# The front block of a fused convolution-attention kernel: angle tables in pieces, a third slot for x, weights issued by ScalarE, and some loads behind the change of blocks

## The reference

```python
xn = _gn(x)                                   # (4, 48, 48, 128), groups of 4 channels
q = xn @ Wq + bq
k = (xn @ Wk + bk) * scaling                  # scaling = 16 ** -0.5
v = xn @ Wv + bv
lepe = depthwise_conv_5x5(v, dw_w) + dw_b
qr = q * cos + rot(q) * sin                   # rot: pairs (a, b) -> (-b, a); cos, sin: (48, 48, 16), one table for all 8 heads
kr = k * cos + rot(k) * sin
attn = einsum("bhnm", qr, kr) + mask          # mask: (8 heads, 2304, 2304), the same for the 4 images
out = softmax(attn) @ v + lepe
x = x + out @ Wo + bo
```

## Time and profile before

| | us |
|---|---|
| median of three runs (lowest, highest) | 3610.34 (3608.89, 3616.03) |
| the profiled execution | 3615.75 |
| its span | 3614.0 |
| front block, from the span's start to the core's first DMA | 168.0 |
| core's first DMA to the first exponential | 13.7 |

### The profile page before, as it was taken

The page is one execution under the profiler, slowest core; times in us unless marked ns, Lnnn a source line. Parts: engine busy times, 40 slices in busy tenths (PEclk is TensorE's granted clock), DMA queues, the critical chain, the costliest instruction groups (busy, mean ns, idle before and its releaser), DMA issues. The chain is left out here.

```text
span 3614.0 us, 96388 instructions
## 1 busy us (share of the span) xinstructions
PE 3426.4 (95%) x30672; PEld 2653.5 (73%) x30672; DVE 2623.8 (73%) x6490; ACT 2029.5 (56%) x3660; POOL 1639.8 (45%) x854
## 2 busy tenths in 40 slices
PE   6599999999999999999999999999399999999988
PEld 4377777777777777777777777777277787877867
DVE  6588888888888888888888888888365564644457
ACT  3366666666666666666666666666145444454533
POOL 4565566565665565556655656566100100005112
PEclk9799999999999999999999999999699999999989
DMA  6732242224224224223322322221511020100011
GB/s 201 243 101 93 91 125 78 93 98 129 67 100 126 94 66 135 91 94 93 109 91 98 103 94 91 99 68 63 167 42 56 24 74 6 37 1 1 1 41 42
DMA packets 111321, 309.50 MB, mean 86 GB/s; under 512 B 11496, under 2 KB 72859, under 8 KB 90299
## 3 DMA queue, kind: packets, MB, share of 16 engines
q1 hardware_dynamic: 111195, 307.85, 27.4%
HBM read 253.49 MB, written 54.31 MB: 85 GB/s over the span
## 5 line engine op out<-in xcount | busy, mean ns | idle before, releaser
L747 DVE CUSTOM_DVE_ANT_0 c_S<-c_Sps,mask_tiles 128x768 f32<-128x768 f32 x1728 | 1619.5, 956 | 425.1 <-PE c_Sps L798 367.0
L688 ACT ACTIVATE c_PT<-c_Tps 128x512 f32<-128x512 f32 x2592 | 1428.7, 605 | 872.0 <-PE c_Tps L809 809.4
L659 POOL TENSOR_SCALAR c_S<-c_S,c_row_max 128x2304 f32<-128x2304 f32 x576 | 1410.9, 2450 | 949.4 <-DVE c_row_max L758 949.4
L809 PE MATMUL c_Tps<-ident,c_S 128*128 128x128 f32 x10368 | 1399.5, 273 | 4.1 <-ACT c_PT L688 4.1
L809 PEld LDWEIGHTS c_Tps<-ident,c_S 128*128 128x128 f32 x10368 | 1226.0, 140 | 151.4 <-ACT c_PT L688 9.9
L798 PE MATMUL c_Sps<-c_K,c_Q 96*128 (+1 forms) x3456 | 853.5, 328 | 43.5 <-DVEq L728 26.3
L822 PE MATMUL c_Ops<-c_PT,c_V 128*32 128x256 f32 x10368 | 619.1, 382 | 0.8 <-ACT c_PT L688 0.8
L822 PEld LDWEIGHTS c_Ops<-c_PT,c_V 128*32 128x32 f32 x10368 | 307.4, 109 | 243.7 <-issue 49.9
L798 PEld LDWEIGHTS c_Sps<-c_K,c_Q 96*128 96x128 bf16 x3456 | 315.0, 98 | 202.7 <-issue 144.4
L1313 DVE TENSOR_SCALAR_CACHE_REDUCE l_S<-l_Sps 128x384 f32<-128x384 f32 x432 | 240.2, 557 | 294.5 <-PE l_Sps L1161 268.2
L1081 ACT ACTIVATE ln2T<-l_Tps 128x384 f32<-128x384 f32 x432 | 196.4, 491 | 403.9 <-PE l_Tps L1182 403.9
(11 more groups left out here) (197 smaller groups left out, 1652.2 us busy)
## 6 DMA issues: line engine op xcount, KB each, us to landing
mask_tiles<-in_mask SPq DMA_DIRECT2D x144, 1152.0 KB, 7.7
numerators<-c_O SPq DMA_DIRECT2D x288, 64.0 KB
ln<-numerators SPq DMA_DIRECT2D x8, 2304.0 KB, 8.4
q_parts<-f_parts SPq DMA_DIRECT2D x12, 576.0 KB, 7.7
k_parts<-f_parts SPq DMA_DIRECT2D x12, 576.0 KB
c_Q<-q_parts SPq DMA_DIRECT2D x71, 96.0 KB
c_vpad<-v_padded SPq DMA_DIRECT2D x8, 756.0 KB, 14.8
c_K<-k_parts SPq DMA_DIRECT2D x7, 864.0 KB, 8.8
```

The costliest lines, as they stand in the source:

```text
L659: pool.tensor_scalar(S[:, slot, :], S[:, slot, :], -1.0, row_max[:, slot:slot + 1], ALU.mult, ALU.add).then_inc(shifted, 1)
L688: act.activation(dst, src, ACT.Exp, scale=-1.0).then_inc(exp_done, 1)
L747: dve.tensor_tensor_reduce(out=S[:, r % ROW_SLOTS, cols(CH, c)].rearrange("p (k n) -> p k n", k=2), in0=Sps[:, n % S_SLOTS, :, 0:GW], in1= ...
L809: last = pe.transpose(Tps[:, g % T_SLOTS, cols(P, k)], S[:, (2 * b + t) % ROW_SLOTS, cols(P, kt)], ident[:, :])
```

## The change

Six edits, all in the front and at the core's start.

1. `XT` has three slots, and x of images 0, 1 and 2 is loaded at the start; x of image 3 when the matmuls of image 0 are done. Each image's x has a semaphore of its own.
2. The angle tables come from the host already repeated for the eight heads, as 128 rows, and are loaded in three pieces each, 384 KB a piece, cos and sin in turn. `with_cos` waits for its own piece.
3. The weights, biases and taps are issued by ScalarE.
4. Two mask tiles and the first-head loads of image 2 leave the front; the core's start issues them. The first-head loads of images 0 and 1 stand half an image later, behind vpad (and behind x of image 3).
5. The statistics are two BN_STATS in each of steps 0, 1 and 2; deviation is in step 3 and normalise in step 4.
6. In the core, TensorE's rows 4 and 6 wait for the loads of image 2 and 3, and ScalarE's second `place_v` for both.

```diff
-        XT = sb("XT", [P, 2, N])
+        X_SLOTS = 3
+        XT = sb("XT", [P, X_SLOTS, N])
@@ front, SyncE
             load_x(0)
-            for i, w in enumerate((a["Wq"], None, a["Wk"], None, a["Wv"])):
...
-            sp.dma_start(cosT[:, :], s["cosT"].unsqueeze(0).to_broadcast([HEADS, D, N])).then_inc(angles_in, 16)
-            sp.dma_start(sinT[:, :], s["sinT"].unsqueeze(0).to_broadcast([HEADS, D, N])).then_inc(angles_in, 16)
+            for c in range(NCH):
+                sp.dma_start(cosT[:, cols(CH, c)], s["cosT"][:, cols(CH, c)]).then_inc(angles_in[c], 16)
+                sp.dma_start(sinT[:, cols(CH, c)], s["sinT"][:, cols(CH, c)]).then_inc(angles_in[c], 16)
             load_x(1)
+            load_x(2)
             for b in range(B):
                 if b:
                     store_parts(b - 1, 1)
                 store_v(b)
-                if b:
-                    load_early(b - 1)
-                sp.dma_start(mask[:, b, :], s["mask"][b]).then_inc(mask_in, 16)
+                if b < 2:
+                    sp.dma_start(mask[:, b, :], s["mask"][b]).then_inc(mask_in, 16)
                 store_parts(b, 0)
                 store_vpad(b)
-                if b + 2 < B:
+                if b + X_SLOTS < B:
                     sp.wait_ge(mm_ready, 2 * STEPS * (b + 1))
-                    load_x(b + 2)
+                    load_x(b + X_SLOTS)
+                if b in (1, 2):
+                    load_early(b - 1)
@@ front, ScalarE: the eight DMAs of weights, biases and taps ahead of its first wait
+                    act.dma_start(weights[:, i, :], w).then_inc(weights_in, 16)
...
-                    if step == STEPS - 2 and b + 1 < B:
+                    if step == 3 and b + 1 < B:
                         deviation(b + 1)
@@ front, VectorE
             def with_cos(u):
                 b, m, c = at(u)
+                if u < NCH:
+                    dve.wait_ge(angles_in[c], 32)
...
-            dve.wait_ge(angles_in, 32)
...
-                    if b + 1 < B and step == STEPS - 1:
+                    if b + 1 < B and step == 4:
                         normalise(b + 1)
                     with_sin(u)
-                    if b + 1 < B and step in (1, 2):
-                        statistics(b + 1, range(NG // 2 * (step - 1), NG // 2 * step))
+                    if b + 1 < B and step < 3:
+                        statistics(b + 1, range(2 * step, 2 * step + 2))
@@ core, SyncE
-            sp.sem_inc(mask_in, 32 * 2)
+            sp.sem_inc(mask_in, 32)
...
+            load_first_head(sp, s, K, Q, V_next, 2, [image_in[2]] * 3)
             load_half(0)
-            load_first_head(sp, s, K, Q, V_next, B - 1, (k_in, q_in, v_in))
-            sp.wait_ge(q_in, 48)
+            load_first_head(sp, s, K, Q, V_next, 3, [image_in[3]] * 3)
+            load_mask(1)
             load_q(1)
@@ core, ScalarE and TensorE
+                elif half:
+                    act.wait_ge(image_in[2], 16 * EARLY_LOADS)
+                    act.wait_ge(image_in[3], 16 * EARLY_LOADS)
...
+                if first and c == 0 and r in (4, 6):
+                    pe.wait_ge(image_in[r // 2], 16 * EARLY_LOADS)
@@ host
-    "cosT": lambda x: x.reshape(N, D).T,
+    "cosT": lambda x: np.tile(x.reshape(N, D).T, (HEADS, 1)),
```

More of the change, by code:

```diff
@@ L356, in v_tokens @@
                 for k in range(GB):
-                    last = pe.matmul(to[:, cols(P, k)], XT[:, b % 2, cols(P, g * GB + k)], weights[:, 4, :],
+                    last = pe.matmul(to[:, cols(P, k)], XT[:, b % X_SLOTS, cols(P, g * GB + k)], weights[:, 4, :],
                                      start=True, stop=True)
@@ L373, in project @@
                 for k in range(2):
[L374 removed]
+                    last = pe.matmul(mm[:, use % MM_SLOTS, k, 0:GW], weights[:, 2 * m + r, :], XT[:, b % X_SLOTS, cols(GW, 2 * c + k)],
                                      start=True, stop=True)
@@ L789, in scores @@
             def scores(ip, p, r, c, first=False):
-                if c == 0 and r == (ROWS - 2 if first else 0):
+                if r == 0 and c == 0 and not first:
                     pe.wait_ge(q_in, 48 * (ip + 1))
                     pe.wait_ge(k_in, 48 * (ip // HEAD_PAIRS + 1))
+                if first and c == 0 and r in (4, 6):
+                    pe.wait_ge(image_in[r // 2], 16 * EARLY_LOADS)
                 n = NCH * r + c
```

42 lines of the change are left out of this document (23 added, 19 removed).

## The result

| | us |
|---|---|
| before, median of four runs (lowest, highest) | 3612.63 (3608.89, 3616.03) |
| changed kernel, median of four runs (lowest, highest) | 3589.63 (3587.29, 3591.86) |
| ratio (95% interval) | 0.9936 (0.9919 to 0.9954) |
| profiled executions, before and after | 3615.75 and 3587.29 |

The change saves 23.0 us; 31 were forecast. The time, 3589.63, is at the upper end of the range, inside it.

The account below looks back on a forecast made before the run. It took late angle tables, waits for x and normalised x, TensorE's rhythm and the store tail to bound the front. 14 + 1.4 + 10.4 + 0 + 6.5 - 1 = 31.3, said 31, off 3610.34: 3579.3 us, range 3571 to 3590.

Parts of the forecast that it names:

- The start: Up to TensorE's third step: tables and x arrive sooner, 14 us less; bounds of the gain 5 and 14.3.
- The pieces: Table loads at the start: fixed parts of pieces overlap, against the skill's 1 MiB rule, which would cost some 3 us.
- Image 0: End of image 0: TensorE's wait for the normalised x goes, 1.4 us less.
- Images 1 and 2: Front's middle images: fewer stalls, 30.3 us becomes 25.5 and 32.1 becomes 26.5, 10.4 less.
- Image 3: Last image of the front: 24.6 us as before, 0 gained.
- The tail: Last matmul to the core's first DMA: moved loads no longer stand there, 6.5 us less, 25.9 becomes 19.4.
- The core's start: After the core's first DMA: vpad lands behind seven issues and VectorE waits, 1 us more; bounds 0 and 5.
- (a): Rival, 24%: eight DMA engines carrying all of k set the front's length; gain 25.5 us, 3585.
- (b): Rival, 12%: x or weights come late at the start, 9 us of it lost; gain 22 us, 3588.
- (c): Rival, 12%: better, images at 24.5 us and the tail less by 9; gain 37 us, 3573.
- (d): Rival, 8%: the core's start gives back 5 us; 3583.
- (e): Rival, 2%: slower, moved loads set the core's start, landing 30 us late, which cancels all.

Follow-up runs that it names:

- e11: e7 with weights, biases and taps issued by SyncE, behind x of image 0 and ahead of the table pieces; 3570.33 us.
- e3: Changed kernel with the tables still in pieces but broadcast by the DMA, 8 heads outermost; 3603.6 us.
- e1: Changed kernel with k laid out in HBM part outermost, so a store is 128 rows on sixteen DMA engines; 3575.29 us.
- e2: Changed kernel with the first-head loads of images 0 and 1 another half image later, behind V of the next image; 3589.0 us.
- e5: Changed kernel with statistics back in steps 1 and 2, deviation in step 4 and normalise in step 5; 3592.8 us.
- e9: Changed kernel with two slots for x instead of three, so x of images 2 and 3 is loaded later; 3607.48 us.
- e12: Changed kernel with two slots for x and also the old, later places of statistics, deviation and normalise; 3599.32 us.
- e4: Changed kernel with two mask tiles and the first-head loads of image 2 back in the front; 3598.8 us.
- e8: e1 with two mask tiles and the first-head loads of image 2 back in the front; 3574.5 us.
- e7: e1 with the core's first DMAs reordered: vpad's half and V of images 2 and 3 first; 3570.29 us.
- e6: e1 with statistics back in steps 1 and 2, deviation in step 4 and normalise in step 5; 3581.4 us.
- e10: e7 with the tables in pieces but broadcast by the DMA, 8 heads outermost; 3580.0 us.

## Why the prediction was right or wrong

**The start: right.** 14 were forecast, 13.2 came (24.15 at the third step, not 23.1). The missing 0.8 is the first projection, 1.1 us later than before. I had the weights sharing engines with x "within a microsecond either way"; e11 shows that they share with the table pieces. The bound below (x late behind slow tables) is what e3 measured at the third step; with the slow step behind it it was 11.5 us, not 8 to 9.

**The pieces: right.** The DMA view of the first 20 us in 40 slices (busy tenths, then GB/s), of the changed kernel:

```profile
DMA  0009159999999999999999999999999999940000
GB/s 0 0 0 111 19 193 350 418 405 399 419 387 377 423 400 398 386 407 408 393 399 393 399 390 442 424 424 396 396 424 424 433 378 406 424 175 0 0 0 0
```

About 400 GB/s from 3.5 us on, with table pieces of 384 KB in it. The Trainium skill's rule of 1 MiB a DMA for 75% of peak (DMA: Bandwidth & Descriptors, Measured (HBM→SBUF, 128 partitions, SWDGE, issued from GpSimd)) rests on DMAs issued by GpSimd. It doesn't hold for these pieces, which SyncE issues one behind another.

**Image 0: right.** 1.4 forecast, 1.2 came. Edit 5's worth is far more than the 1.4 of that place: 4.4 in all with edit 1.

**Images 1 and 2: wrong in image 2.** Image 1 took 24.7 where I said 25.5; image 2 took 30.9 where I said 26.5. The step that failed is "for image 2 I add 1: mask and first-head loads of image 1 are queued ahead of its k stores on engines that are then always busy". Where I added 1 us, it took 5.4 more than the 25.5. Half of the mechanism was right: the engines that carry k are always busy, and e1, which takes the stores off these eight, has images that begin every 24.4 us. The other half, the loads ahead of k in the queue, is not the cause: e2 moved them, and the waits for k were 11.5 us instead of 11.0. The waits for k were 2.2, 7.6 and 1.3 us, not 0.9 an image. I had taken 0.7 us, the only such wait before, as the measure of how near the stores were. It was small because each of images 0 to 2 was held up elsewhere, by tables, x or normalise, so that the stores had 30 to 32 us an image to land in. Once those waits went, an image asked for them in 24.5. Experiments that bring such waits back bear this out: ScalarE waits 4.7 us for k in e5, 3.2 in e9 and 1.0 in e12.

**Image 3: 0 forecast, 1.7 longer.** Its own wait for a store reached TensorE with 0.67 us, as before. But it began behind the 4.07 us stop, at half clock. Eight matmuls took 4.54 us there (96.19) against 2.75 at 20.23.

**The tail: 6.5 forecast, 4.8 came.** With the loads put back (e4) the tail is 6.4 us longer, which is the forecast's term of 6.5; why the tail of the changed kernel is still 1.7 longer than the 19.4 forecast stays open. Late k stores of image 2 don't reach into it: ScalarE's wait for them ended at 118.9, ahead of the last matmul. Edit 4 as a whole I had at 6.5 and something of image 2; e4 puts it at 11.5 on this kernel.

**The core's start: right.** 1 forecast, 0.7 came by the first DMA. Its weak point, vpad behind seven loads, cost VectorE 1.53 us (1 forecast).

**The sum.** 31.3 less 23.8 is 7.5: 3.5 in images 1 and 2, 1.7 in image 3, 1.7 in the tail, 0.8 at the start and 0.2 in image 0, less 0.3 at the core's start and a rounding. The medians differ by 23.0, not 23.8, and the forecast used 31, not 31.3, so 8.0 of the gain are missing. Another 2.3 us are the level: with a fourth run the median of before was 3612.63 and not 3610.34. Together that is the 10.3 between 3579.3 and 3589.63. The range held the time because it was wide enough for rival (a).

**The rivals.** (a) came nearest to what happened. It gave a gain of 25.5, 3585 and an end of the stores at 140.5 (the core's first DMA is at 143.60), and its signs, longer waits of ScalarE for stores and a last matmul past 120 (122.45), both showed. I gave it 24% against 40%. The evidence I weighed against it, the single wait of 0.7 us, was worth little, and its arithmetic, 20.3 MB through eight engines over the whole front, should have led. One reading in it is wrong: 163 GB/s is not near what k alone gets at the end, which is 209; that it was the right rate for the mixture, e8 shows. And (a) is not the whole account: by it alone e5 would have cost under 1.5 us and e9 at most 4, and they cost 4.4 and 16.3. So a wait of TensorE for x or for the normalised x still lengthens the front, although the stores are short of engines. (b), weights late, was there but for 1 us. (c), (d), (e) and (f) were not seen.

**Not settled.** The later blocks of the two profiled executions differ by 5 us without a cause that I can name; nothing was run on them. Edits 1 and 5 on e7, one at a time, were not run, so the worths of 16.3 and 4.4 hold for k on eight engines only; e6 is the one measure of edit 5 on sixteen (6.3).

## What to carry to other kernels

A store that nobody waits for today can be near to being waited for: work out for the set of DMA engines that carries it how many bytes it must move per image, and compare that with the pace you are about to reach, not with the present one. Look at the outermost dimension of each large DMA, stores as well as loads; changing a layout in HBM from 8 x 16 rows to 128 rows gave 14 us here, at the price of three more DMA issues a head. And a wait in an in-order queue is priced by what stands behind it: moving work earlier (the statistics) is a gain only if its input is moved earlier too.

## What the runs showed of the hardware that was not expected

- The same 3.0 MB of loads cost 11.5 us with k on eight DMA engines (e4) and nothing with k on sixteen (e8), while the mean share over images 2 and 3 was 0.85 and 0.86 in the one and 0.98 and 1.03 in the other (it can read over 1). A mean share of 0.86 left no room for k.
- Small DMAs on a queue of their own are not ahead of large ones that another queue issues at the same time. The weights, 0.2 MB, held the first projection to between 14.19 (e7) and 14.94 us (e4), 14.60 in the changed kernel, beside 384 KB pieces, and to 17.32 (e3) and 17.20 (e10) beside pieces on eight engines; with the weights issued ahead of them on one queue it was at 13.58 (e11).
- After TensorE had stood for 4.07 us in the changed kernel its granted clock was 0.50 (the lower of its two levels, 1.2 GHz) from 94 to 98 us and 1.00 (2.4 GHz) from 100 us:

```profile
94.00:96.00 2.00, 1.25 (x2) 0.83 (x3) 0.00 (x0) 2.00 (x5) 1.70 (x2) 0.50 0.36 116
96.00:98.00 2.00, 2.00 (x4) 1.01 (x3) 0.00 (x0) 1.83 (x3) 2.00 (x2) 0.50 0.77 248
...
100.00:102.00 2.00, 2.00 (x16) 1.74 (x15) 1.81 (x3) 0.51 (x2) 0.74 (x1) 1.00 1.13 432
```

So a stall of 4.07 us in front of a step cost 1.7 us more behind it; in e9 the steps behind stops of 6.01 and 10.02 us took 5.12 and 5.42 us for the same eight matmuls (clock 0.50 from 55 to 59 and from 92 to 96 us). A short stop can do it too, and need not: behind a stop of 1.41 us at the same place a step took 2.85 us in e6 and 4.54 in e12 (clock 0.59 and 0.56 from 34 to 38 us).
